# Routed rows stored contiguously, combined by 128 indirect gathers, with 24 shared units behind the routed ones

## What is computed

```python
shared = _expert(x, Wg_s, Wu_s, Wd_s)          # silu(x Wg^T) * (x Wu^T) Wd^T, inner width 256
probs = sigmoid(x @ Wr.T + rb)                 # 8 experts
scores, idx = top_k(probs, 2)
out = shared
for e in range(8):
    out = out + cw[..., e:e + 1] * _expert(x, Wg[e], Wu[e], Wd[e])
x = _layernorm(x + out)
```

## Time and profile before

| | us |
|---|---|
| median of 3 runs | 1071.56 |
| fastest, slowest | 1067.3, 1071.86 |
| span of the profiled execution | 1167.6 |
| attention and routing, to | 667 |
| 8 shared units with the weights, to | 711 |
| 24 shared units and the transition, to the first routed tanh | 776 |
| 72 routed units, to the last tanh | 1064 |
| results, to the end | 1168 |

### The profile page before, as it was taken

One profiled execution on the slowest core, in us unless ns is written; L12 is line 12 of the kernel. 1 busy time (PEld: TensorE's weight loads), 2 busy tenths in 40 slices (PEclk: granted clock), 3 DMA queues, 4 the chain that ended last, 5 costly groups with the idle time before them and its releaser, 6 DMA issues. The chain is left out here.

```text
span 1167.6 us, 25490 instructions
## 1 busy us (share of the span) xinstructions
PE 862.4 (74%) x7726; PEld 527.1 (45%) x7727; DVE 742.3 (64%) x1965; ACT 591.6 (51%) x915; POOL 665.4 (57%) x1076
## 2 busy tenths in 40 slices
PE   3699999989999999989997359977666677764000
PEld 2435455444544444444443247755555456653000
DVE  3646797678776777778773539965454545453543
ACT  1367776657666666767674125533343434343223
POOL 4246586777786867877766382005444444455543
PEclk9589999789997898989888579988988997897555
DMA  5000010011101110111001223422222222220554
GB/s 158 10 10 10 20 42 29 33 38 41 34 25 45 36 36 18 45 36 38 22 30 44 67 84 101 117 74 67 65 60 65 59 57 62 60 68 24 153 150 126
DMA packets 99944, 65.93 MB, mean 56 GB/s; under 512 B 9341, under 2 KB 93703, under 8 KB 99889
## 3 DMA queue, kind: packets, MB, share of 16 engines
q1 hardware_dynamic: 82672, 43.97, 13.7%
q0 software_dynamic: 8768, 17.07, 4.5%
q10 hardware_dynamic: 8448, 4.20, 1.2%
HBM read 34.50 MB, written 31.74 MB: 57 GB/s over the span
## 5 line engine op out<-in xcount | busy, mean ns | idle before, releaser
L669 ACT ACTIVATE probs<-S 128x1024 f32<-128x1024 f32 x320 | 325.2, 1032 | 147.0 <-PE S L449 92.9
L351 POOL TENSOR_SCALAR_AFFINE_SELECT probs<-probs 128x256 f32<-128x256 f32 (+2 forms) x576 | 247.8, 459 | 154.7 <-ACT probs L669 153.7
L1235 POOL DMA_INDIRECT z_scratch<-y,rows x144 | 145.4, 1009 | 221.3 <-ACT y L1370 191.6
L449 PE MATMUL S<-qkT 32*128 32x512 f16 (+3 forms) x1024 | 192.1, 321 | 21.8 <-PE S L449 15.8
L464 PE MATMUL O<-probs,v_aug 128*32 128x512 f32 (+3 forms) x2048 | 191.4, 496 | 2.6 <-POOL probs L351 2.6
L1378 ACT ACTIVATE th<-S 128x512 f32<-128x512 f32 x104 | 62.4, 600 | 214.6 <-remote 110.7
L1452 DVE SCALAR_TENSOR_TENSOR gated<-th,S 128x512 f32<-128x512 f32 x104 | 70.9, 682 | 153.6 <-ACT th L1378 140.6
L1295 PE MATMUL O<-w_T,hid 128*128 (+1 forms) x1248 | 104.0, 236 | 86.0 <-DVE hid L1469 83.9
L232 POOL DMA_INDIRECT rows_scratch<-xrow,slot_i x128 | 131.1, 1025 | 39.7 <-issue 31.1
L1273 PE MATMUL S<-xT_rt,w_T 128*128 128x256 f16 x864 | 127.4, 301 | 14.8 <-issue 12.9
L1295 PEld LDWEIGHTS O<-w_T,hid 128*128 128x128 f16 x1248 | 85.8, 105 | 110.1 <-issue 84.4
(11 more groups left out here) (154 smaller groups left out, 1261.9 us busy)
## 6 DMA issues: line engine op xcount, KB each, us to landing
rows<-rows_scratch SPq DMA_DIRECT2D x72, 130.0 KB, 2.3
z<-z_scratch SPq DMA_DIRECT2D x32, 256.0 KB, 3.6
x_in<-in_L_attn_x ACTq DMA_DIRECT2D x16, 256.0 KB, 2.8
x_scratch<-x SPq DMA_DIRECT2D x16, 256.0 KB
x1T_scratch<-x1T SPq DMA_DIRECT2D x16, 256.0 KB, 2.0
xT_sh<-x1T_scratch SPq DMA_DIRECT2D x32, 128.0 KB
x_in<-x_scratch SPq DMA_DIRECT2D x32, 128.0 KB
out<-res SPq DMA_DIRECT2D x16, 256.0 KB, 2.4
```

Of the source, the lines that this page charges most:

```text
L351: pool.affine_select(out=v, in_=v, compare_op=ALU.is_ge, fill=0.0, base=0, pattern=[[0, n], [1, P]], channel_multiplier=-1).then_inc(maske ...
L449: mm = pe.matmul(S[(g + c) % 2][:, col:col + T - kb * P], k, q, start=True, stop=True)
L669: act.activation(probs[:, g % 2, c, :], S[(g + c) % 2][:, :], ACT.Exp, scale=-SCALE / SPLIT_UP ** 2).then_inc(s_exp, 1)
L1235: pool.indirect_dma_start(out=z_dram, in_=y[:, r, a, :], in_offset=None, out_offset=bass.IndirectOffsetOnAxis(ap=rows[:, r, a, P + 1:P + 2 ...
```

## The change

Rows in `rows_scratch` lose the score and the place (`ROW` is 128). DVE keeps scores and slots per token in `token_score` and `token_slot`. A routed unit's `y` is no longer scaled (ACT copies it in one operation) and goes to `y_scratch` at the unit's own place by a plain store from SP, issued eight units later in SP's order; the load of a unit's rows waits for the transposes of the unit eight before.

Only the 8 early shared units stand ahead of the routed ones. The other 24 follow as `late` units, written out. Once the table is made, GpSimd turns slots into rows of `y_scratch` (15 operations), waits for all stores of y, and then gathers, batch by batch, two rows per token: 8 indirect DMAs of 128 rows a batch, 128 in all, at most four batches ahead of DVE's sums. `result(b)` multiplies by the score and adds (8 operations), takes the statistics and computes 1/std on DVE by a chain of small operations in place of GpSimd's power; ACT writes the result and issues its store. `result(0)` to `result(9)` stand behind every second late unit from the fifth on, the other six behind the last.

```diff
-ROW = P + 2
+ROW = P
...
-        xrow = sb("xrow", [P, 2, NT, 2, ROW])
+        xrow = sb("xrow", [P, 2, NT, ROW])
+        token_slot = sb("token_slot", [P, 2, NB * NT])
+        token_score = sb("token_score", [P, 2, NB * NT])
...
-                        out=rows_dram, in_=xrow[:, par, t, k, :], in_offset=None,
+                        out=rows_dram, in_=xrow[:, par, t, :], in_offset=None,
...
-                tail = xrow[:, par].rearrange("p t k w -> p k t w")
-                dve.tensor_scalar(tail[:, :, :, P], rmax[:, :, :], 1.0 / (UP * H_UP), None, ALU.mult)
-                chain(dve.tensor_copy(tail[:, :, :, P + 1].bitcast(I32), place_i[:, :, :]))
-                dve.tensor_scalar(place_i[:, :, :], place_i[:, :, :], T, None, ALU.add)
+                dve.tensor_scalar(token_score[:, :, bass.ds(NT * c, NT)], rmax[:, :, :], 1.0 / (UP * H_UP), None, ALU.mult)
...
+                dve.tensor_copy(token_slot[:, :, bass.ds(NT * c, NT)], slot_f[:, :, :])
...
-        def over_units(eng, body):
+        def over_units(eng, early, routed, late, result):
             R = NRING
-            for u in range(R):
-                body(u, u, u, 0, True)
-            with eng.Fori(1, NSH // R) as i:
-                for r in range(R):
-                    body(R * i + r, R * i + r, r, i, True)
-            for u in range(R):
-                body(NSH + u, u, u, 0, False)
+            for n in range(EARLY):
+                early(n)
+            for n in range(R):
+                routed(EARLY + n, n, n, 0)
             with eng.Fori(1, NRT // R - 1) as i:
                 for r in range(R):
-                    body(NSH + R * i + r, R * i + r, r, i, False)
+                    routed(EARLY + R * i + r, R * i + r, r, i)
             for r in range(R):
-                body(NSH + NRT - R + r, NRT - R + r, r, NRT // R - 1, False)
-        assert NSH % NRING == 0 and NRT % NRING == 0
...
+                routed(EARLY + NRT - R + r, NRT - R + r, r, NRT // R - 1)
+            b = 0
+            for n in range(EARLY, NSH):
+                late(NRT + n, n, n % R)
+                if n >= RESULT_FROM and (n - RESULT_FROM) % 2 == 0:
+                    result(b)
+                    b += 1
+            late(None, None, None)
+            for b in range(b, NB):
+                result(b)
+        RESULT_FROM = EARLY + 4
...
+            def store_y(n, r):
+                sp.wait_ge(y_ready, n + 1)
+                sp.dma_start(y_dram[bass.ds(n * UNIT, UNIT)].rearrange("(a p) w -> p a w", p=P), y[:, r])\
+                    .then_inc(y_out[r], 16)
+            def routed(u, n, r, i):
...
-                if not (isinstance(i, int) and i == 0):
-                    sp.wait_ge(z_out[r], 2 * 16 * i)
+                first = isinstance(i, int) and i == 0
+                if not first:
+                    sp.wait_ge(xT2_full, n - NRING + 1)
                 at = sp.value_load(unit_row[0:1, bass.ds(n, 1)], min_val=0, max_val=TAIL)
                 sp.dma_start(rows[:, r], rows_dram[bass.ds(at, UNIT)].rearrange("(a p) w -> p a w", p=P))\
                     .then_inc(rt_in[r], 16)
-            over_units(sp, body)
...
+                if not first:
+                    store_y(n - NRING, r)
+            def late(u, n, r):
+                if n == EARLY:
+                    for r in range(NRING):
+                        store_y(NRT - NRING + r, r)
+                if n is not None and n + NRING < NSH:
+                    load_shared(n + NRING)
+            def early(n):
+                load_shared(n)
...
+            def routed_then_shared(u, n, r, i):
+                if isinstance(n, int) and n == NRT - NRING:
+                    for m in range(EARLY, EARLY + NRING):
+                        load_shared(m)
+                routed(u, n, r, i)
+            over_units(sp, early, routed_then_shared, late, lambda b: None)
...
+            slots_of = token_slot[:, :, :].rearrange("p k j -> p (k j)")
+            for e in range(1, NE):
+                ins = pool.tensor_scalar(shift_f[:, e - 1, :], slots_of, float(e * CAP), G[:, e - 1:e], ALU.is_ge, ALU.mult)
+            chain(ins)
+            for e in range(1, NE):
+                chain(pool.tensor_tensor(slots_of, slots_of, shift_f[:, e - 1, :], ALU.subtract))
+            chain(pool.tensor_copy(token_row[:, :], slots_of))
+            for r in range(NRING):
+                pool.wait_ge(y_out[r], 16 * (NRT // NRING))
+            for b in range(NB):
+                r = b % ZRING
+                if b >= ZRING:
+                    pool.wait_ge(tot_done, b - ZRING + 1)
                 pool.sem_inc(parted, 1)
-                for a in range(2):
-                    pool.indirect_dma_start(
-                        out=z_dram, in_=y[:, r, a, :], in_offset=None,
-                        out_offset=bass.IndirectOffsetOnAxis(ap=rows[:, r, a, P + 1:P + 2].bitcast(I32), axis=0),
-                        bounds_check=2 * NTOK - 1, oob_is_err=False).then_inc(z_out[r], 16)
-            over_units(pool, body)
...
+                for k in range(2):
+                    for t in range(NT):
+                        pool.indirect_dma_start(
+                            out=z[:, r, k, t, :], in_=y_dram, out_offset=None,
+                            in_offset=bass.IndirectOffsetOnAxis(ap=token_row[:, NTILE * k + NT * b + t:NTILE * k + NT * b + t + 1], axis=0),
+                            bounds_check=NRT * UNIT - 1, oob_is_err=False).then_inc(z_in[r][k], 16)
...
-                act.wait_ge(rt_in[r], 16 * (i + 1))
-                for a in range(2):
-                    ins = act.activation(y[:, r, a, :], O[r % 2][:, a * P:(a + 1) * P], ACT.Copy,
-                                         scale=rows[:, r, a, P:P + 1])
-                ins.then_inc(y_ready, 1)
-            def body(u, n, r, i, shared):
+                act.wait_ge(down_full, EARLY + n + 1)
+                if not (isinstance(i, int) and i == 0):
+                    act.wait_ge(y_out[r], 16 * i)
+                act.copy(y[:, r].rearrange("p a d -> p (a d)"), O[r % 2][:, 0:UNIT]).then_inc(y_ready, 1)
...
+            def late(u, n, r):
+                if n is None:
+                    high_half(NU - 1, NRING - 1)
+                    return
+                tanh(u, r)
+                high_half(u - 1, r - 1)
+                m = NRT - 3 + n - EARLY
+                if m < NRT:
+                    send(m, m % NRING, m // NRING)
+            def result(b):
+                par = b % 2
+                act.wait_ge(shift_done, b + 1)
+                if b >= 2:
+                    act.wait_ge(res_out[par], 16 * (b // 2))
+                for t in range(NT):
+                    ins = act.activation(res[:, par, t, :], acc[:, NT * b + t, :], ACT.Identity,
+                                         scale=rstd2[:, par, t:t + 1], bias=shift2[:, par, t:t + 1])
+                ins.then_inc(res_done, 1)
+                act.wait_ge(res_done, b + 1)
+                act.dma_start(out[bass.ds(b, 1)].rearrange("a (t p) d -> p (a t) d", p=P), res[:, par])\
+                    .then_inc(res_out[par], 16)
...
+            def late(u, n, r):
+                if n is None:
+                    low_half(NU - 1, (NU - 1) % 2)
+                    for m in range(NSH - 3, NSH):
+                        add_shared(m)
+                    return
+                gate(u, r % 2)
+                if n >= EARLY + 3:
+                    add_shared(n - 3)
+                low_half(u - 1, 1 - r % 2)
+                hidden(u, r % 2)
+            def inverse_root(r):
+                chain(dve.tensor_scalar(var2[:, :], meanvar2[:, :, 1], EPS, None, ALU.add))
+                dve.tensor_scalar(nhalf2[:, :], var2[:, :], -0.5, None, ALU.mult)
+                chain(dve.tensor_scalar(root2[:, :].bitcast(I32), var2[:, :].bitcast(I32), 1, None,
+                                        ALU.logical_shift_right))
+                chain(dve.tensor_scalar(r.bitcast(I32), root2[:, :].bitcast(I32), -1.0, float(0x5f3759df),
+                                        ALU.mult, ALU.add))
+                for _ in range(3):
+                    chain(dve.tensor_tensor(root2[:, :], r, r, ALU.mult))
+                    chain(dve.tensor_tensor(root2[:, :], root2[:, :], nhalf2[:, :], ALU.mult))
+                    chain(dve.scalar_tensor_tensor(out=r, in0=root2[:, :], scalar=1.5, in1=r, op0=ALU.add, op1=ALU.mult))
+            def result(b):
+                r, par = b % ZRING, b % 2
+                dve.wait_ge(acc_done, 2 * b + 2)
+                for k in range(2):
+                    dve.wait_ge(z_in[r][k], 16 * NT * (b // ZRING + 1))
+                    if k:
+                        dve.wait_ge(first_done, b + 1)
+                    for t in range(NT):
+                        j = NT * b + t
+                        ins = dve.scalar_tensor_tensor(out=acc[:, j, :], in0=z[:, r, k, t, :], scalar=token_score[:, k, j:j + 1],
```

(16 more changed lines are left out.)

299 lines of the change are left out of this document (118 added, 181 removed).

## The result

The changed kernel took 1105.76 us (median of four, 1104.85 to 1106.83) beside 1071.71 for the kernel before (four, 1067.3 to 1074.27): ratio 1.032, 95% interval 1.028 to 1.035, slower as forecast (1099). So two questions follow: where the 34 us came from, and why those runs take them back. Every ratio here compares undisturbed executions only (some take a per cent or two longer at a lower granted clock), while the medians beside it hold all of them, so the two need not divide exactly.

The account below looks back on a forecast made before the run. The prediction took GpSimd's scatters to bound the routed stage at 2.62 us a unit. Start -58, routed units -10 and tail +95 gave +27 on 1071.6, so 1099 us, with an 8 in 10 range of 1050 to 1125.

Parts of the forecast that it names:

- the order of the engines in the tail: After the routed units: VectorE's results set the end at 199 us, GpSimd's gathers stay ahead, the last landing near 182.
- The start: Up to the first routed tanh: at 718 instead of 776.39, 58 us earlier, as 24 shared units move away.
- The missing 96 us: Profiled span 1167.6 against slowest timed run 1071.86; taken as routed-stage holes that are mostly a cost of being profiled.
- the pace before: Routed stage of the kernel before: scatters set 2.62 us a unit, bounded at 2.54 to 2.69.
- Rival (b): Faster, 1051 us: half the missing 96 us lies in attention, so a routed unit before cost 3.30 us; chance 0.17.
- the sign: Whole kernel: slower by 27 us; turns to faster at 0.38 us more per routed unit, a pace before of 3.0.
- Routed units: Routed stage: 72 units at 2.45 us, 176.4 us instead of 186.0, a gain of 10.
- The tail: From first late tanh to the end: 199 us where 103.8 stood, +95.
- detour over ACT: After each of ten results in the late units: VectorE stands still 2.9 us until ACT's next tanh.
- The interference rule: Late units: a two-port VectorE copy shuts GpSimd out; without such copies gathers at 1.27 us and an end of 1084.
- rows 6: Scatter timings in the routed stage: 1.12 us overlapping the unit's fp16 copy, 0.97 without, cited as bearing on the rule.

Follow-up runs that it names:

- those runs: Later runs of the unedited changed kernel beside the kernel before, on chip B: 1155.5 us beside 1159.3, ratio 0.993.
- B: One of three chips of the follow-up runs; there the kernel before took 1159.3 us and the unedited changed kernel 1155.5, ratio 0.993.
- A: One of three chips of the follow-up runs; there the kernel before took 1170.9 us.
- C: One of three chips of the follow-up runs; there the kernel before took 1167.2 us.

## Why the prediction was right, and where it was not

The range and the order of the engines in the tail were right. The start and the routed stage came out in the sum partly by luck.

*The missing 96 us.* They are no cost of the profile. The first trace came from a condition in which long rows of indirect DMAs starve the other engines, the times from one in which they don't. But they do not all lie in the routed stage, as the prediction took it. Attention's last 16 scatters run in a row beside the first shared units, in both kernels. In the first trace ACT waits there 12.41 us before the second tanh for something nameless, though the matmuls for it had ended at 675.33:

```profile
673.86 1.47 PE L1273 MATMUL S<-xT_sh,w_T 128*128 128x256 f16 x12
690.13 0.60 ACT L1378 ACTIVATE th<-S 128x512 f32<-128x512 f32 x1 [12.41 <-remote]
```

In the changed kernel's trace of the result the same two tanhs stand 2.69 us apart:

```profile
661.94 0.60 ACT L1385 ACTIVATE th<-S 128x512 f32<-128x512 f32 x1 [0.97 <-PE S L1262]
```

The first seven steps take 36.4 us in the first trace and 20.1 here. In the kernel before the other shared units follow without a gap, and SyncE issues the padding stores (757.92) only behind their last loads, so these 16 us should delay its routed stage by as much. In the changed kernel the table is waited for anyway (45.7 us from first shared to first routed tanh here, 45.9 on B). In twelve further traces, all of A, B and C, the first of these steps takes 13.5 to 18 us. Attention may hold another 14 us: the first shared tanh stands at 673.0 in the first trace and at 659.3 in the result's.

So the pace before that I derived, 2.54 to 2.69 us, does not stand. An estimate: a span of 1071.7 - 2.3 = 1069.4, less the 880.2 us that the first trace spends outside the stage, plus the 16 us and up to 14, leaves 206 to 219 us for 71 steps, 2.9 to 3.1 each. No trace of the kernel before in the condition of its timed runs exists to check it. Without scatters 2.61 was measured. Rival (b), that part of the missing time lies outside the stage and a scattered unit costs more, was thus partly true in the result; it did not turn the sign, because most of what lies outside fell to the kernel before alone. On A, B and C a unit costs more by far, 3.98 us in the trace on B. By the two traces on B the change saves 64 us to the first routed tanh and 282.4 - 193.2 = 89 us in the routed stage, and the new tail costs 238.5 - 100.5 = 138 us more: 15 us saved, in the timed runs 8 (ratio 0.993).

*The 34 us.* With these estimates: tail 203.8 - 103.8 = +100; first shared to first routed tanh 45.7 us instead of 103.4 - 16.4 = 87.0, -41; attention and the routed stage together -25. The last two rest on the first trace, less what starves in it; the tail's 203.8 is measured in the result.

The Trainium skill (Runtime: NRT & Kernel Launch, section on the launch sequence) puts 9 to 15 us around a kernel; 1.8 to 2.4 us lay between span and time in the runs compared, so that estimate did not hold for this measure.

*The start.* First shared to first routed tanh 45.7 us, forecast 45, but not by the forecast's path. I had the last weights (713.5) set it, with the rows just ahead (713.3). In the result the weights are split at 683.4 and the units then stand still until GpSimd's table is ready at 696.9 and the rows have come. In the first trace the two met because the row of 16 scatters had held the weights up. That the first routed tanh stood at 704.9 and not at 718 is attention: the first shared tanh moves between 659 and 690 us over fourteen traces, with a granted clock in this stretch of 0.88 in the earliest and 0.85 in the latest. The result's is the earliest, and the only one without starving, so which of the two shortened it is open. I gave that no width.

*Routed units: 194.4 instead of 176.4.* The mis-sized term. The straight steps are 2.3 and 2.5 us, as forecast. But every eighth and its neighbour take 3.1 to 3.6, 2 us for each turn of the loop, in the kernel before without scatters as well (tanhs at 837.80, 840.24, 843.64, 846.75). What in the turn costs them was not tested. The earlier trace rows showed three steps, none of them across a loop's end. The other 6.5 us are SyncE's: I had named no issue for the 16 loads put ahead of a routed unit's rows, though I had their kind (8.38 us for eight stores) in a row.

*The tail: 203.8, forecast 199.* Term by term: first gather 8.8 us after the first late tanh (9.8); gathers 1.30 apart (1.31); result 6.5 to 6.8 (6.3), the 13 small operations 0.20 apart as forecast, the multiply-adds 2.4 instead of 2.2; detour over ACT 2.83 (2.9); round 13.85 (13.5); GpSimd's last gather lands near 1086, 187 after the start (182). The order of the engines was right: VectorE's results with the wait for ACT behind each set the pace, GpSimd stayed ahead. Only VectorE's result is 0.4 us dearer than forecast, ten times over and six times more at the end.

*The sum.* Forecast by stretches 718 + 176.4 + 199 + 5.4; measured 704.9 + 194.4 + 203.8 + 1.8 (with the time's median 0.8 higher). Two errors of 13 and 18 us of opposite sign made 1105.8 look closer to 1099 than the sum deserved: that is luck. So is the -58 for the start, which was about -41 in the condition of the timed runs, while the gain of 10 in the routed stage was more like 11 to 25; the total before, being given, hid both.

*The interference rule* (the Trainium skill, SBUF — State Buffer, "Who interferes with whom"). It would have given gathers at 1.27 us beside units without an fp16 copy. They were 1.02 us long in the mean and 1.30 apart, so no difference showed. Nor do rows 6 bear on the rule as the prediction has it: the scatter of 0.97 us (856.77) also ran beside such a copy, and the copy reads PSUM, so that it runs in a two-port mode at all is not shown.

```profile
856.70 0.42 DVE L1432 COPY xT_rt<-W 128x512 f16<-128x512 f16 x1
```

The dearer interference here runs the other way, from GpSimd to the others.

## What to carry to other kernels

Ask of a change in two halves what each is worth: the order with the old finish stood at 0.970, while the gathers brought a longer finish (6.8 us a result instead of 1.7) onto the engine that already set the pace. When a profile and the timed runs disagree by a tenth, find which condition each belongs to before pricing anything with either, and time both kernels on more than one chip. A block of loads put ahead of a queue's next urgent one makes that one wait for every issue: 16 loads of about 0.6 us each cost 6.5 us here. A subtraction that gives a stage its time from another run's trace holds only if everything else in the trace ran alike; one stretch that both kernels share, such as the first shared units here, can test that.
